# A six-row sampling window, a sparse stage for the offsets outside it, and row additions shared out anew

## The reference, cut to what matters

```python
sy = off[:, :, :, 0] + kys[None, None, :, None, None] + hh[None, None, None, :, None]
sx = off[:, :, :, 1] + kxs[None, None, :, None, None] + ww[None, None, None, None, :]
y0f = jnp.floor(sy)
x0f = jnp.floor(sx)
...
val = gather(y0, x0, (1 - dy) * (1 - dx)) + gather(y0, x0 + 1, (1 - dy) * dx) + gather(y0 + 1, x0, dy * (1 - dx)) + gather(y0 + 1, x0 + 1, dy * dx)
patches = val.reshape(Bx, C, KK, Hx, Wx)
out = jnp.einsum('bikhw,oik->bohw', patches, weight.reshape(Cout, Cin, KK))
```

## Time and profile before

| | us |
|---|---|
| median of 3 runs (13377.7 to 13395.6) | 13394.25 |
| profiled execution, its span | 13389.0 |
| first stage, until the sampling stage starts | 0 to 474.9 |
| `sample_and_convolve` | 474.9 to 8549.7 |
| all that comes after | 8549.7 to 13389.0 |

### The profile page before, as it was taken

The page is one execution under the profiler, slowest core; times in us unless marked ns, Lnnn a source line. Parts: engine busy times, 40 slices in busy tenths (PEclk is TensorE's granted clock), DMA queues, the critical chain, the costliest instruction groups (busy, mean ns, idle before and its releaser), DMA issues. The chain is left out here.

```text
span 13389.0 us, 237451 instructions
## 1 busy us (share of the span) xinstructions
PE 12626.2 (94%) x81086; PEld 10422.1 (78%) x81086; DVE 11629.7 (87%) x15744; ACT 11084.4 (83%) x13077; POOL 6971.2 (52%) x3614
## 2 busy tenths in 40 slices
PE   7899999999999999999999999988089989999999
PEld 4799999999999999999999999743053345555555
DVE  4699999999999999999999999778987878888888
ACT  2588888888888888888888888539777889899898
POOL 0255555555555555555555555303320068888887
PEclk9999999999999999999999999779599999999999
DMA  4666667667666667766766666754464433333332
GB/s 122 162 178 177 178 178 178 178 178 178 178 178 178 178 177 178 178 178 177 177 178 178 177 178 178 189 149 153 136 173 143 156 111 104 99 106 104 100 104 85
DMA packets 824757, 2102.23 MB, mean 157 GB/s; under 512 B 83236, under 2 KB 430810, under 8 KB 681562
## 3 DMA queue, kind: packets, MB, share of 16 engines
q1 hardware_dynamic: 754082, 2029.60, 56.7%
q10 hardware_dynamic: 69495, 57.45, 1.5%
HBM read 1818.07 MB, written 268.74 MB: 156 GB/s over the span
## 5 line engine op out<-in xcount | busy, mean ns | idle before, releaser
L518 PE MATMUL dc_p<-dc_t 96*128 96x144 f32 x51948 | 6846.0, 285 | 21.1 <-PEq L515 20.8
L585 POOL TENSOR_TENSOR dc_t<-dc_t 128x648 f32<-128x648 f32 x2885 | 4526.4, 1569 | 4021.9 <-POOLq L584 3977.9
L518 PEld LDWEIGHTS dc_p<-dc_t 96*128 96x128 f32 x51948 | 6529.5, 189 | 42.4 <-issue 21.5
L645 DVE TENSOR_TENSOR dc_t<-dc_p,dc_t 128x1296 f32<-128x1296 f32 x2886 | 4342.9, 1505 | 507.3 <-DVEq L643 444.5
L464 ACT ACTIVATE dc_t<-dc_t 96x1152 f32<-96x1152 f32 x2892 | 3590.1, 1241 | 463.6 <-ACTq L488 462.3
L466 ACT ACTIVATE dc_t<-dc_t 96x1152 f32<-96x1152 f32 x2892 | 3367.8, 1165 | 347.5 <-ACTq L465 10.4
L2161 DVE TENSOR_TENSOR_SCAN ms_t<-ms_t,ms_p 128x512 f32<-128x512 f32 x1728 | 2127.7, 1271 | 282.8 <-PE ms_p L2103 204.6
L2077 POOL TENSOR_TENSOR ms_t<-ms_t 128x1536 f32<-128x1536 f32 x576 | 1987.8, 3456 | 503.5 <-DVE ms_t L2161 499.7
L2113 PE MATMUL ms_p<-ms_t,top_t 128*128 128x512 f32 x3456 | 1774.7, 596 | 0.0
L559 PE MATMUL dc_p<-dc_t 128*128 128x180 f32 (+1 forms) x7488 | 1633.5, 318 | 17.0 <-PEq L554 10.9
L2103 PEld LDWEIGHTS ms_p<-top_t,ms_t 128*128 128x128 f32 x6912 | 849.7, 141 | 967.6 <-issue 693.8
(11 more groups left out here) (210 smaller groups left out, 9397.4 us busy)
## 6 DMA issues: line engine op xcount, KB each, us to landing
dc_t<-sxd SPq DMA_DIRECT2D x1446, 864.0 KB, 5.7
ms_t<-bcd SPq DMA_DIRECT2D x576, 256.0 KB, 3.3
dc_t<-xrT SPq DMA_DIRECT2D x145, 675.0 KB, 8.2
kvd<-wk_t SPq DMA_DIRECT2D x18, 1536.0 KB, 5.1
szd<-mi_t SPq DMA_DIRECT2D x36, 768.0 KB, 4.3
xvd<-mi_t SPq DMA_DIRECT2D x36, 768.0 KB, 4.8
dld<-mi_t SPq DMA_DIRECT2D x36, 768.0 KB, 3.4
ms_t<-dld SPq DMA_DIRECT2D x36, 768.0 KB, 6.7
```

The source lines that it names most:

```text
L518: ins = e.matmul(PT[j % 2][:, t // 3, (t % 3) * 144:(t % 3 + 1) * 144], HX[:, m // 2 % RP, m % 2, t * 128:(t + 1) * 128], XW[:, i, ky:ky + ...
L585: e.tensor_tensor(z[:, :, 0:HALF], z[:, :, 0:HALF], z[:, :, HALF:2 * HALF], ALU.add)\
L645: e.tensor_tensor(Zt[:, n % 4, :].rearrange("p (b m i) -> p b m i", b=3, i=CG), PT[n % 2][:, :, 0:432].rearrange("p b (m i) -> p b m i", i ...
```

## The change

**Six rows.** `WIN` goes from 8 to 6: a sampling matmul has 108 columns instead of 144, `weigh` 972 elements instead of 1296, the y hats 6 rows. The loads of picture rows shrink from 10 to 8 rows a tile.

**A sparse stage.** Offsets outside the smaller window (further than `REACH` = 2.5 from its middle) are treated one by one. In the first stage ScalarE takes |y offset - middle| (`size`), VectorE finds the 8 largest of each partition and chunk and their places (`largest`, two instructions in place of two reductions), and SP clears a correction tensor `cor` of 36864 x 180 floats with 96 transfers. A new phase `far_samples` then picks up to 128 such samples (at most 8 in a partition), fetches by indirect DMA their offsets, four pixels and weight rows, works out what each adds to the result, and scatters that to `cor`. If there are more, the window loop runs 17 times instead of once. In the inputs of the reference, 67 samples lie outside, at most 5 in one partition.

**Correction and sums.** GpSimd starts each tile's `ACC` from `cor` (`keep`: a `tensor_scalar` and a `tensor_tensor` on 128x360), in place of the factor in L620.

**Three row additions.** Six rows are added as 3 + 3 by GpSimd (`halve`, 486 elements, now into `ZH`), then row 0 + row 1 by GpSimd (`top`, 162 elements, one group behind `halve`), then + row 2 by VectorE for two groups at once (`sum_rows`, 324 elements). `quarter` is gone.

**Hats in pairs.** ScalarE's Abs and Relu each cover both groups of an `HX` slot (96x2304 instead of 96x1152), the Abs one pair ahead of the Relu.

**Stores.** `store_tile` moves from ScalarE to SP, behind the fourth `pair_load` of a tile, and stores the tile two back. The tensor `fd` is shifted by one tile for that.

```diff
-WIN = 8
-NWIN = 13
+WIN = 6
+NWIN = 17
...
+                def size(c):
+                    e.wait_ge(s_oy, c + 1)
+                    if c >= 3:
+                        e.wait_ge(s_mx, c - 2)
+                    for u in range(3):
+                        ins = e.activation(AB[:, c % 3, u * CM:(u + 1) * CM], OY[:, c % 2, u, :], ACT.Abs,
+                                           bias=DT[:, u:u + 1])
+                    ins.then_inc(s_ab, 1)
...
+                    if c >= 2:
+                        largest(c - 2)
...
+def far_samples(nc, k):
...
+                e.wait_ge(s_oh, 1)
+                for n in range(NCAND):
+                    ins = e.matmul(PB[:, 0:4], OH[:, n, :], PAY[:, n, :], start=(n == 0), stop=(n == NCAND - 1))
+                ins.then_inc(s_pay, 1)
+                e.wait_ge(s_rd, 1)
+                e.matmul(PA[:, 0:128], ONES[:, :], RD[:, :], start=True, stop=True).then_inc(s_r, 1)
+                e.wait_ge(s_em, 1)
+                e.matmul(PO[:, 0:CM], EM[:, :], OUT[:, :], start=True, stop=True).then_inc(s_o, 1)
...
+                e.wait_ge(s_ad, 1)
+                gather(YX[:, 0:1], k.d["oyd"].rearrange("b y x (c o) -> (b y x c) o", o=1), 0, s_yx)
+                gather(YX[:, 1:2], k.d["sxd"].rearrange("b t v k (x o) -> (b t v k x) o", o=1), 1, s_yx)
+                gather(WG[:, :], k.d["w_gat"], 2, s_wg)
+                e.wait_ge(s_ix, 1)
+                for n in range(4):
+                    gather(XV[:, n, :], k.d["xrT"][0:B * ROWS].rearrange("r x (g i) -> (r x g) i", i=CG), 4 + n, s_xv)
+                e.wait_ge(s_go, 1)
+                e.indirect_dma_start(k.d["cor"], bass.IndirectOffsetOnAxis(ap=AD[:, 3:4], axis=0), SUMS[:, :], None)\
+                    .then_inc(s_cor, 16)
+                e.wait_ge(s_cor, 16)
...
                 def tile_load(i, b, first):
-                    e.dma_start(XW[:, i % 2, :, :], k.d["xrT"][b, DS(first, WIN + 2)].rearrange("r p c -> p r c"))\
+                    e.dma_start(XW[:, i % 2, :, :], k.xr_v[b][DS(first, WIN + 2)].rearrange("r p c -> p r c"))\
                         .then_inc(s_xw[i % 2], 16)
 
                 def row_loads(i, b, ti, y):
                     e.dma_start(OYT[:, i % 2, :], k.oyd_v[b, DS(y, 1)].rearrange("a p c -> (a p) c")).then_inc(s_row[i % 2], 16)
                     e.dma_start(TAB[:, i, :],
                                 k.d["c_tab"][DS(ti, 1)].rearrange("a p c -> (a p) c")).then_inc(s_row[i % 2], 16)
+
+                def kept_loads(i, b, ti, y):
+                    e.dma_start(CR[:, i, :], k.cor_v[DS(b * NT + y, 1)].rearrange("a p c -> (a p) c")).then_inc(s_cr[i % 2], 16)
+                    e.dma_start(KF[:, i:i + 1],
+                                k.d["c_keep"][DS(ti, 1)].rearrange("a p c -> (a p) c")).then_inc(s_cr[i % 2], 16)
+
+                def store_tile(i, at, sem):
+
+                    e.wait_ge(s_out, 2).then_inc(s_out, -2)
+                    dst = k.d["fd"][DS(at, 1)].rearrange("y c (h p) x -> p (c h) (y x)", p=HM)
+                    e.dma_start(dst, FT[:, i % 2, :, :]).then_inc(sem, 16)
 
...
                         first = e.snap(near * (y + ((y * 43) >> 7)) + w * WIN + s0)
                         ti = e.snap(t0 + w + y * NWIN)
                         row_loads(i, b, ti, y)
+                        kept_loads(i, b, ti, y)
                         for q in range(10):
                             pair_load((10 * i + q) % RP, b, y, q)
                             if q == 0:
                                 tile_load(i, b, first)
+                            if q == 3:
+                                done = b * NT + y if i >= 2 else e.snap(((w + 15) >> 4) * NRB + (b * NT + y))
+                                store_tile(i, done, s_st[i % 2])
...
-                def hats(m):
-
-                    q, u = m // 2 % RP, m % 2
-                    if u == 0:
-                        e.wait_ge(s_bx[q], 16).then_inc(s_bx[q], -16)
-                    e.activation(HX[:, q, u, :], HX[:, q, u, :], ACT.Abs, bias=QX[:, 0:1]).then_inc(s_ab, 1)
+                def distance(q):
+
+                    e.wait_ge(s_bx[q % RP], 16).then_inc(s_bx[q % RP], -16)
+                    e.activation(HX[:, q % RP, :, :], HX[:, q % RP, :, :], ACT.Abs, bias=QX[:, 0:1]).then_inc(s_ab, 1)
+
+                def hats(q):
+
                     e.wait_ge(s_ab, 1).then_inc(s_ab, -1)
-                    e.activation(HX[:, q, u, :], HX[:, q, u, :], ACT.Relu, bias=1.0, scale=-1.0).then_inc(s_hx, 1)
+                    e.activation(HX[:, q % RP, :, :], HX[:, q % RP, :, :], ACT.Relu, bias=1.0, scale=-1.0)\
+                        .then_inc(s_hx, 2)
...
+                distance(0)
+                for q in range(AHEAD // 2):
+                    distance(q + 1)
+                    hats(q)
 
                 def body(b, y2, w):
                     for n in range(NBB):
                         i, j = n // NB, n % NB
-                        if j == 3:
-                            y = y2 * NRB + i
-                            done = b * NT + y if i else e.snap(((w + 15) >> 4) * NRB + (b * NT + y))
-                            store_tile((i - 1) % NRB, done, s_st[(i - 1) % 2])
-                        hats((n + AHEAD) % NBB)
+                        if n % 2 == 0:
+                            distance((n + AHEAD) // 2 + 1)
+                            hats((n + AHEAD) // 2)
                         if j in (4, 5, 9, 10):
                             row_weights((i + 1) % 2, (4, 5, 9, 10).index(j))
...
                     for t in range(TAPS):
                         ky = t // 3
-                        ins = e.matmul(PT[j % 2][:, t // 3, (t % 3) * 144:(t % 3 + 1) * 144],
+                        ins = e.matmul(PT[j % 2][:, t // 3, (t % 3) * WIN * CG:(t % 3 + 1) * WIN * CG],
                                        HX[:, m // 2 % RP, m % 2, t * 128:(t + 1) * 128],
                                        XW[:, i, ky:ky + WIN, g * CG:(g + 1) * CG],
                                        start=True, stop=True)
...
                 def halve(n):
 
                     z = Zt[:, n % 4, :].rearrange("p (t m) -> p t m", t=TAPS)
-                    if n >= 2:
-                        if n % 2:
-                            e.wait_ge(s_sum, 1).then_inc(s_sum, -1)
-                            e.sem_inc(s_va, 2)
-                        else:
-                            e.wait_ge(s_qt, 1).then_inc(s_qt, -1)
+                    if n >= 3 and n % 2:
+                        e.wait_ge(s_sum, 1).then_inc(s_sum, -1)
+                        e.sem_inc(s_va, 2)
                     e.wait_ge(s_z, 1).then_inc(s_z, -1)
-                    e.tensor_tensor(z[:, :, 0:HALF], z[:, :, 0:HALF], z[:, :, HALF:2 * HALF], ALU.add)\
+                    e.tensor_tensor(ZH[:, n % 4, :, :], z[:, :, 0:HALF], z[:, :, HALF:2 * HALF], ALU.add)\
+                        .then_inc(s_low, 1)
+
+                def top(n):
+
+                    e.wait_ge(s_low, 1).then_inc(s_low, -1)
+                    e.tensor_tensor(ZH[:, n % 4, :, 0:CG], ZH[:, n % 4, :, 0:CG], ZH[:, n % 4, :, CG:2 * CG], ALU.add)\
                         .then_inc(s_half, 1)
+
+                def keep(i):
+
+                    e.wait_ge(s_cr[i % 2], 32).then_inc(s_cr[i % 2], -32)
+                    e.tensor_scalar(ACC[:, i, :, :], ACC[:, i, :, :], KF[:, i:i + 1], None, ALU.mult).then_inc(s_pre, 1)
+                    e.wait_ge(s_pre, 1).then_inc(s_pre, -1)
+                    e.tensor_tensor(ACC[:, i, :, :], ACC[:, i, :, :], CR[:, i, :].rearrange("p (v c) -> p v c", v=2),
+                                    ALU.add).then_inc(s_acc, 1)
 
                 def body(b, y2, w):
                     for n in range(NBB):
                         halve(n + 5)
...
-                for n in range(5):
+                        top(n + 4)
+                        if n % NB == 2:
+                            keep(n // NB)
+
+                halve(0)
+                for n in range(1, 5):
                     halve(n)
+                    top(n - 1)
                 loops(e, body)
...
                     e.wait_ge(s_f, 1).then_inc(s_f, -1)
                     total = k.SUM[:, b, conv, :]
                     e.tensor_tensor(total, total, PF[:, conv * CM:(conv + 1) * CM], ALU.add)
+                    if conv == 0:
+                        e.wait_ge(s_acc, 1).then_inc(s_acc, -1)
                     a = ACC[:, i, conv, :]
-                    e.scalar_tensor_tensor(out=a, in0=a, scalar=TAB[:, i, WIN:WIN + 1],
-                                           in1=PF[:, conv * CM:(conv + 1) * CM], op0=ALU.mult, op1=ALU.add).then_inc(s_ff, 1)
+                    e.tensor_tensor(a, a, PF[:, conv * CM:(conv + 1) * CM], ALU.add).then_inc(s_ff, 1)
...
-                    hy = HY[:, i, :, :].rearrange("p c r -> p (c r)")[:, j * 72:(j + 1) * 72]
+                    hy = HY[:, i, :, :].rearrange("p c r -> p (c r)")[:, j * 9 * WIN:(j + 1) * 9 * WIN]
                     e.tensor_tensor(
```

(25 more changed lines are left out.)

380 lines of the change are left out of this document (310 added, 70 removed).

## The result

| | before | after |
|---|---|---|
| median, us | 13385.98 (4 runs, 13370.84 to 13395.60) | 12902.51 (4 runs, 12897.67 to 12907.61) |
| span of the profiled execution | 13389.0 | 12905.0 |
| until the sparse phase or, before, the sampling stage starts | 0 to 474.9 | 0 to 476.8 |
| the sparse phase | none | to 540.7 |
| `sample_and_convolve` | 474.9 to 8549.7 (8074.8) | 540.7 to 8065.8 (7525.1) |

The ratio is 0.9643, 95% interval 0.9631 to 0.9655: faster by 483 us. The forecast was 12755 with a range of 12580 to 13040; the time came out 148 us above the forecast, inside the range. It lies above the forecast's own ends, though (12646 to 12866): the range held by the room that was left for rival B. Between the two profiled executions the sampling stage gives back 549.7 us, and 65.9 us lie between the old and the new start of it: 549.7 - 65.9 = 483.8, and the spans differ by 484.0.

A forecast was written before the change was run, and what follows sets the result against it. TensorE was taken to bound the sampling stage at 2.786 us a group. 13389 less 710 us for shorter passes plus 73 for the sparse phase gave 12752; the median stood 5 above the profile, so 12755, range 12580 to 13040.

The forecast's parts named there:

- rival B: Sampling stage: GpSimd's additions and hand-overs with VectorE set the pace, 2.60 us a group; 12926, up to 13040 us; chance 0.18.
- own ends: Whole kernel: the sum with its terms at their extremes, 12646 to 12866 us, narrower than the stated range.
- The load of the weights: Sampling matmul: loading 128 weight columns sets the pass, 0.1222 to 0.1085 us, saving 0.247 us a group, 710 us.
- my upper end: Sampling stage: at 0.110 us a pass the gain is 633 us; with a 110 us sparse phase, 12866 us.
- "TensorE doesn't notice" `keep`: GpSimd's `keep` delays `sum_rows` some 1.3 us, without TensorE noticing: over 1 us until the next `weigh` input is ready.
- The 0.586 us "which the change leaves alone": TensorE, sampling stage: transposes and convolution matmuls take 0.586 of a group's 2.786 us, unchanged.
- The sparse phase: Between first stage and sampling: adds 73 us, between 45 and 110; small instructions 0.25 us each, gather waits 12 us.
- The other engines: Sampling stage, per group: ScalarE 2.21, VectorE 1.79, GpSimd 1.86 us, all under 2.54; DMA share 0.77.
- The ring: GpSimd waits for `sum_rows` before every second `halve`, `sum_rows` for two `top`s: 2.35 us a group, 0.19 under 2.54.
- Rival A: Sampling matmul: streamed columns set the pass, 0.092 us; 12206 to 12350 us; chance 0.12.
- rivals C and D: C: GpSimd's loop above 2.76 us a group, 13646 at 2.85; D: window loop runs 17 times; together 0.06.

## Why the prediction was right, and where it was off

The mechanism was right: from a width between 144 and 126 streamed columns downwards the load of 128 weight columns sets the sampling pass, and the gain from it is less than half of what the columns promise. The runs with 7 rows, 6 rows and 96 weight columns show it each in its own way. The sum came out 153 us too low for the profiled execution (12752 against 12905.0), past the upper of its own ends, 12866. That the time lies within the range is owed to the room for rival B, whose mechanism didn't happen, so that part is luck. By its steps:

- **The load of the weights, the mis-sized term.** I took 0.1085 us a pass from the one-column matmuls at 1.2 GHz, halved and scaled by the weight columns, 0.107 to 0.110. Measured are 0.1110 by the way in which the prediction reads a row, just outside. From the blocks in the timelines a group's 18 passes fell by 0.22 us, which is 634 us for 2880 groups instead of 710: 76 us less, the gain that I had given for my upper end. The changed kernel at its own start shows what the halving misses. At clock 0.50, the timeline of TensorE:

```profile
566.46 23.35 PE L828 MATMUL dc_p<-dc_t 96*128 96x108 f32 x108 [31.85 <-PEq L825]
589.60 0.42 PE L858 MATMUL dc_p<-top_t,dc_t 128*128 128x128 f32 x1
```

  (589.60 - 566.46) / 108 = 0.214 us a pass. Half of that is 0.107; at full clock it is 0.1106. The pass does not quite halve with the clock, so here the row from the lower clock gave a lower bound, not a middle. The scaling by weight columns was an assumption as well: the earlier trace rows have one width only and can't show it. The run with 96 columns agrees with it (0.1106 x 96/128 = 0.083 us, below its 0.0928) but doesn't measure it.
- **"TensorE doesn't notice" `keep`.** Wrong, by 43 us. The waits of the changed kernel show them, and the run with `keep` on VectorE gives back 41. The step that failed is that `sum_rows` "has over 1 us until its next `weigh` input is ready": in a usual group the wait ahead of `weigh` is 0.96 us, beside a step of the y hats 0.20, `sum_rows` was 1.50 us late where 1.3 were forecast, and behind `weigh` stands the `unload` that TensorE waits for.
- **The 0.586 us "which the change leaves alone".** By the two timelines 0.53 became 0.55 for a group with two transposes: by readings that are rounded, 0.01 to 0.02 us, 29 to 58 us over the stage. No run takes it apart.
- **The start of the stage.** TensorE's first sampling pass comes 566.46 - 540.74 = 25.7 us after the stage's start, 8 more than the 17.7 before. I had no term for it. ScalarE's timeline shows the reason:

```profile
555.88 2.21 ACT L777 ACTIVATE dc_t<-dc_t 96x2304 f32<-96x2304 f32 x1 [0.18 <-ACTq L776]
562.09 2.21 ACT L777 ACTIVATE dc_t<-dc_t 96x2304 f32<-96x2304 f32 x1 [4.00 <-ACTq L776]
564.21 2.11 ACT L782 ACTIVATE dc_t<-dc_t 96x2304 f32<-96x2304 f32 x1
```

  The Abs now runs one pair ahead, so the first Relu stands behind the second Abs, and that one waits 4.00 us for its load. From the first Abs to TensorE's first pass it is 10.6 us, and 2.7 before. With the hats one group at a time (the run above) it is 560.91 - 557.70 = 3.2 us again, and the first pass comes 19.2 us after the stage's start instead of 25.7.
- **The clock behind the sparse phase.** In the changed kernel TensorE starts the stage at clock 0.50 and stays there until 600 us, 33.5 us of work at half speed, some 17 us lost. I had no term for it. The kernel before loses as much at its start in another way: its first 108 passes take 16.3 us, where 108 x 0.1228 = 13.3 is the steady rate, and a little later TensorE stands still:

```profile
531.13 1.54 PE L559 MATMUL dc_p<-dc_t 128*128 128x180 f32 x4 [10.76 <-PEq L554]
```

  VectorE waits 11.25 us just before, for a tile's y offsets (L609), with the DMA share at 1.03. With two slower stretches behind the wait, that makes some 16 us too. The changed kernel has no such wait. The two nearly cancel, which is luck; no run takes them apart.
- **The sparse phase.** Forecast 73, measured 65.9 between the two starts of the sampling stage and 65 by the run without it. The small instructions were cheaper (0.19), the waits for gathers 4.5 instead of 12, the strided sum dearer.
- The terms add up: 76 for the pass, 43 for `keep`, 29 for the rest of the group at 0.01 and 8 for the start, less 7 for the phase, are 149, for a miss of 153. A reading of two decimals times 2880 groups is good to 14 us. The windows say the same: 2.592 instead of 2.540 us a group are 150 us, and what the stage holds beyond 2880 such groups went from 50 to 61 us.
- **The other engines.** VectorE 1.79 and ScalarE 2.20 us a group came as forecast. GpSimd's prices were too high: `halve` 1.069 us instead of 1.225, `top` 0.486 instead of 0.535, `keep`'s first half 1.18, its second 0.95 (0.957). First stage and DMA share (0.76 for 0.77): as forecast.
- **Rival B** had 12926, which is nearer to 12903 than my forecast, but not by its mechanism. The ring does not set the pace: GpSimd is idle 1106 us of 3000 while it waits for VectorE, TensorE is busy 99.7%, and with 96 weight columns the same ring runs at 2.36 us a group. Only its smallest part is real, the ring's delay at `keep`.
- **Rival A** would have needed a load under 90 ns, and the pass is 0.1106 us; **rivals C and D** didn't happen.

## What to carry to other kernels

Before narrowing a matmul's streamed side, find what its weight load costs at the clock of the stage: below it no column saves anything. Here only the first row taken away shortened the pass, and sampling matmuls of five rows left the clock at its lower level and made the program take half as long again. Where an engine has slack on average, look for the longest single detour on it, here 2.1 us once in 20 groups, and follow it through every queue behind the one that waits, to the engine that sets the pace. And an engine that helps out is judged at the pace that results, not at the one before.

## What the runs showed of the hardware

**The clock with a load-bound TensorE.** With 90 or 54 streamed columns and 128 weight columns the granted clock was 0.50 in the middle of the stage, though TensorE was busy 3000 of 3000 us; with 108 columns it was 1.00. All of them had come into the stage at 0.50. A full TensorE in the profile is no proof of a full clock. At the start of the sampling stage the clock comes up at different times in different executions of nearly the same program: in the window from 600 to 660 us it was 0.99 in the changed kernel, 1.00 with `top` on VectorE and 0.66 with single hats.

**Additions on VectorE and GpSimd wait for each other.** In the run with `top` on VectorE, the timeline of the two engines:

```profile
4002.17 2.12 POOL L892 TENSOR_TENSOR dc_t<-dc_t 128x486 f32<-128x486 f32 x2 [2.74 <-POOLq L891]
...
4003.38 1.27 DVE L974 TENSOR_TENSOR dc_t<-dc_t 128x324 f32<-128x324 f32 x1
...
4008.50 1.54 POOL L892 TENSOR_TENSOR dc_t<-dc_t 128x486 f32<-128x486 f32 x1 [0.41 <-POOLq L891]
4008.63 0.48 DVE L974 TENSOR_TENSOR dc_t<-dc_t 128x324 f32<-128x324 f32 x1
```

At 4003.38 `top` starts while two `halve`s run until 4004.29, and it takes 1.27 us, until 0.36 us behind their end. At 4008.63 it takes 0.48, and now the `halve` beside it takes 1.54 instead of 1.06. `weigh`, which reads one operand from PSUM, stays at 1.17 throughout. The Trainium skill, "SBUF — State Buffer", section "SBUF: two separate sides", has the two engines share a pair of ports as an exclusive lock when a VectorE instruction has two SBUF inputs and a GpSimd one reads SBUF too; the one that starts first holds it for its whole instruction. The rows agree in that one of the two is held up by about what the other takes. In the second pair it is the `halve` that is held up, though its record starts 0.13 us earlier; by these records, whose times are rough on GpSimd, the order doesn't come out as the page has it. The addition costs VectorE 0.819 us on average here and 1.108 in the run with 96 weight columns, where 0.48 is what it takes when it isn't held up; that is what made VectorE the limit there.

**GpSimd's price isn't one line.** 162 elements take 0.486 and 486 take 1.069 us, 1.80 ns an element; between 648 and 1536 it was 2.12. The additions of 648 were in place and those of 486 are not; whether that is the reason wasn't tried.
